# Every operation of a fused two-block transformer kernel gets a new place in its engine's queue

## What is computed

```
x = x + tanh(g0) * cross_attention(layernorm(x), ctx)        8 heads, rotary q and k, 128 context rows
x = x + tanh(g1) * bitlinear(relu(h)^2, w_proj)              h = bitlinear(ln(x), w_fc) + gate * low_rank(ln(x))
x = x + tanh(g2) * (ln(x) @ W1.T + mean(ctx) @ W2.T + b)
x = x + tanh(g3) * bitlinear(gelu(bitlinear(ln(x), w1, b1)), w2, b2)   activations rounded to 8 bits
```

## Time and profile before

| | |
|---|---|
| median of 3 runs | 1177.76 us (1174.64 to 1179.39) |
| span of the profiled execution, first to last instruction | 1176.7 us |
| PE, DVE, ACT, POOL busy, share of the span | 93%, 81%, 68%, 50% |
| chain that ended last: PE, ACT, DVE, POOL, issue, DMA | 55%, 17%, 16%, 5%, 4%, 2% |
| mean granted TensorE clock | 0.978 |

### The profile page before, as it was taken

The page is one execution under the profiler, slowest core; times in us unless marked ns, Lnnn a source line. Parts: engine busy times, 40 slices in busy tenths (PEclk is TensorE's granted clock), DMA queues, the critical chain, the costliest instruction groups (busy, mean ns, idle before and its releaser), DMA issues.

```text
span 1176.7 us, 22172 instructions
## 1 busy us (share of the span) xinstructions
PE 1094.3 (93%) x8270; PEld 677.4 (58%) x8558; DVE 953.5 (81%) x1989; ACT 799.4 (68%) x1575; POOL 591.5 (50%) x567
## 2 busy tenths in 40 slices
PE   5776699999999999999899999999999999999997
PEld 5544456474655656475655656475656656564654
DVE  4796868778789888788878798898879886998667
ACT  3988947676683958576584857676674957586545
POOL 4243545464653746454544656555545555564431
PEclk9888799999999999999999999999999999999999
DMA  9959651434525343533625252443436242432210
GB/s 339 367 153 309 204 122 47 99 81 77 126 59 117 69 116 73 104 81 68 126 53 136 57 123 68 89 110 77 108 55 145 45 119 61 103 69 55 68 45 27
DMA packets 273802, 128.11 MB, mean 109 GB/s; under 512 B 247568, under 2 KB 248080, under 8 KB 272016
## 3 DMA queue, kind: packets, MB, share of 16 engines
q1 hardware_dynamic: 273136, 125.73, 41.8%
q10 hardware_dynamic: 560, 0.96, 0.3%
HBM read 57.19 MB, written 8.39 MB: 56 GB/s over the span
## 4 chain that ended last, share of the span: by engine, by line
PE 55%; ACT 17%; DVE 16%; POOL 5%; issue 4%; DMA 2%; SPq 0%; ACTq 0%; DVEq 0%
PE ps L1861 14%; PE ps L1835 10%; PE ps L1904 6%; PE ps L1920 5%; PE ps L1788 5%; ACT e L966 4%; PE ps L1735 4%; PE ps L1883 4%; ACT rl L1002 3%; ACT hid L1007 2%; ACT sq L1013 2%; PE ps L1760 1%; DVE st L1369 1%; PE ps L1841 1%; PE ps L1775 1%
## 5 line engine op out<-in xcount | busy, mean ns | idle before, releaser
L1835 PE MATMUL ps<-xT,fcT 128*128 128x256 f16 x2048 | 262.5, 276 | 10.8 <-ACT rl L1002 7.1
L749 POOL TENSOR_TENSOR rs<-ve,nhalf 128x1 f32<-128x1 f32 x160 | 101.7, 638 | 306.1 <-DVE ve L1374 222.8
L1861 PE MATMUL ps<-pjT,hid 128*128 128x512 fp8e4 x1024 | 232.3, 379 | 2.6 <-POOL hid L776 1.6
L1835 PEld LDWEIGHTS ps<-xT,fcT 128*128 128x128 fp8e4 x2048 | 200.1, 99 | 52.6 <-ACT rl L1002 10.0
L776 POOL TENSOR_TENSOR hid<-sq,hid 128x512 f16<-128x512 f32 x128 | 163.1, 1279 | 80.3 <-ACT sq L1013 79.4
L1861 PEld LDWEIGHTS ps<-pjT,hid 128*128 128x128 f16 x1024 | 98.0, 98 | 98.3
L1002 ACT ACTIVATE rl<-ps,rsf 128x256 f32<-128x256 f32 x256 | 106.4, 469 | 25.0 <-PE ps L1841 24.8
L966 ACT ACTIVATE e<-ps,nmb,sig 128x128 f32<-128x128 f32 x256 | 113.1, 462 | 7.2 <-DVE nmb L1412 6.9
L1904 PE MATMUL ps<-w1T,q4T 128*128 128x512 fp8e4 x480 | 114.2, 379 | 0.7 <-issue 0.6
L1058 ACT ACTIVATE q<-h 128x2048 f16<-128x2048 f32 x30 | 57.3, 1910 | 79.3 <-DVE h L1531 79.3
L781 POOL TENSOR_TENSOR e<-e,einv 128x512 f32<-128x512 f32 x64 | 70.1, 1100 | 78.5 <-DVE einv L1416 78.5
(11 more groups left out here) (243 smaller groups left out, 2025.7 us busy)
## 6 DMA issues: line engine op xcount, KB each, us to landing
xb<-in_x SPq DMA_DIRECT2D x16, 512.0 KB, 3.6
xa<-in_x SPq DMA_DIRECT2D x15, 512.0 KB, 4.0
...
h<-in_w1T SPq DMA_DIRECT2D x6, 1024.0 KB, 5.8
h<-in_w2T SPq DMA_DIRECT2D x6, 1024.0 KB, 6.4
h<-in_wkvT SPq DMA_DIRECT2D x2, 1024.0 KB, 12.6
hid<-in_w_fc SPq DMA_DIRECT2D x2, 1024.0 KB, 9.9
```

Source lines behind the costliest of these rows:

```text
L1835: pe.matmul(ps[:, FFN0 + m % 2, a * G:(a + 1) * G], fcT[:, k, f * P:(f + 1) * P], xT2[:, xs, k, :], start=(xs == 0 and k == 0), stop=False)
L1861: mm = pe.matmul(ps[:, FFN0 + t, :], hid[:, xs, c, t * P:(t + 1) * P], pjT[:, c, :], start=(c == 0 and xs == 0), stop=(c == FC - 1 and xs ...
```

## The change

Every number in `ORDER` and `PREP` may be another; nothing else differs. No instruction, buffer or wait is added or removed. Counted over the queues of before and after: 340 of 658 operations of PE stand at another rank in their queue, 616 of 837 of DVE, 328 of 554 of ACT, 449 of 552 of POOL and 264 of 338 of SP. Most moves are by one to three ranks; `add_b2` on POOL moves by up to 26 and the load of b1 on SP by 28. The diff, cut to what the prediction speaks of:

```diff
@@ PE
-                s=((13,), (31,), (60,), (106,), (146,), (182,), (221,), (261,), (299,), (335,), (374,), (412,),
+                s=((13,), (31,), (61,), (105,), (146,), (183,), (220,), (261,), (300,), (337,), (373,), (412,),
...
-                    (173, 180, 183, 185, 186, 191, 192, 195), (212, 218, 220, 223, 224, 228, 230, 232),
+                    (173, 179, 181, 184, 185, 187, 192, 193), (212, 217, 222, 223, 225, 226, 227, 231),
...
-                    (331, 334, 340, 341, 342, 344, 346, 351), (370, 373, 378, 382, 383, 384, 385, 386),
+                    (331, 334, 339, 340, 345, 346, 347, 348), (370, 376, 378, 379, 380, 382, 385, 386),
...
-                w2=((92, 107), (132, 145), (170, 178), (210, 222), (247, 264), (288, 302), (326, 336), (364, 377),
+                w2=((91, 106), (131, 145), (170, 182), (210, 221), (247, 264), (287, 301), (327, 338), (366, 375),
@@ ACT
-                exp=((22, 23, 26, 27), (55, 56, 58, 60), (90, 98, 101, 102), (127, 128, 129, 134),
-                     (159, 160, 162, 167), (188, 190, 191, 192), (221, 222, 224, 226), (254, 255, 256, 261),
+                exp=((23, 24, 26, 27), (57, 58, 60, 63), (91, 92, 102, 103), (126, 127, 134, 135),
+                     (160, 161, 165, 167), (190, 191, 193, 194), (221, 222, 225, 229), (255, 256, 257, 263),
...
-                x2_hi=((50, 51), (84, 85), (113, 114), (144, 145), (176, 178), (207, 208), (240, 241), (272, 273),
+                x2_hi=((43, 54), (85, 86), (114, 115), (144, 145), (178, 179), (208, 209), (241, 242), (272, 273),
@@ POOL
-                add_b2=((57, 63), (93, 102), (123, 132), (155, 165), (195, 206), (222, 238), (261, 272), (295, 302),
-                        (329, 336), (363, 370), (398, 404), (427, 438), (461, 472), (501, 506), (527, 529),
+                add_b2=((67, 72), (108, 122), (141, 145), (171, 185), (209, 210), (245, 246), (264, 294), (297, 314),
+                        (340, 341), (364, 397), (398, 429), (431, 440), (469, 477), (507, 512), (528, 529),
@@ PREP
             PE=dict(x3_turn=(632, 634), q4_turn=(638, 642), q5_turn=(648, 649, 650, 651, 653, 654, 655, 656),
-                    k=(2, 3), v=(5, 6), low=(0,), mix=(14,), tern=(4, 10, 11, 15, 19, 20, 21, 22), low_t=(16,),
-                    row_scale=(24,), mean=(30,), spread=(1, 8, 12, 18, 25)),
+                    k=(2, 3), v=(5, 6), low=(0,), mix=(14,), tern=(4, 9, 11, 16, 18, 19, 20, 21), low_t=(23,),
+                    row_scale=(27,), mean=(30,), spread=(1, 10, 12, 15, 26)),
...
-                    thr=(9, 15, 20, 37, 46, 48, 49, 52), wo_max=(12,), v_top=(22,), wo_scale=(26,), wo_lo=(30,),
-                    mix_row=(43,), low_rank=(42,), v_parts=(28,), wx_max=(53,), hidden=(54,), wx_scale=(58,),
-                    wx_lo=(88,), row_scale=(56,), mean=(71,), diag=(55,), round=(72, 78, 81, 89, 90, 95, 97, 101),
-                    clip=(79, 85, 86, 91, 94, 98, 100, 103)),
+                    thr=(6, 13, 18, 34, 44, 45, 47, 48), wo_max=(20,), v_top=(24,), wo_scale=(25,), wo_lo=(29,),
+                    mix_row=(51,), low_rank=(39,), v_parts=(52,), wx_max=(50,), hidden=(55,), wx_scale=(67,),
+                    wx_lo=(88,), row_scale=(62,), mean=(70,), diag=(56,), round=(72, 73, 81, 86, 90, 91, 98, 102),
+                    clip=(76, 80, 87, 92, 94, 97, 114, 129)),
...
-                    evac=(6, 14, 15, 29, 33, 35, 36, 37), rows=(4, 7, 10, 21), whole=(5, 8, 12, 28), low=(32,),
-                    wx=(46,), sums=(39, 40, 41, 42, 43, 44, 45, 47), lift=(54, 61, 62, 67, 71, 76, 79, 80)),
+                    evac=(7, 14, 16, 30, 34, 35, 36, 37), rows=(4, 8, 10, 22), whole=(6, 11, 13, 29), low=(42,),
+                    wx=(53,), sums=(39, 40, 41, 44, 45, 46, 47, 49), lift=(55, 56, 64, 67, 74, 79, 81, 83)),
...
-            SP=dict(u=(0,), rows=(16,), ctx=(2,), wk=(3,), wq=(1,), wv=(7,),
-                    piece=(4, 5, 10, 18, 19, 15, 22, 24, 27, 29, 31, 32, 33, 36, 37, 38, 40, 41, 45, 47, 48, 50, 52, 55),
-                    wo=(6,), wc=(14,), wx=(13,), b1=(17,)))
+            SP=dict(u=(1,), rows=(15,), ctx=(0,), wk=(4,), wq=(2,), wv=(7,),
+                    piece=(3, 5, 9, 16, 14, 22, 21, 18, 26, 28, 30, 31, 32, 35, 36, 37, 38, 39, 43, 44, 46, 49, 52, 55),
+                    wo=(8,), wc=(20,), wx=(19,), b1=(45,)))
```

More of the change, by code:

```diff
@@ L336, in build @@
             PE=dict(
[L337 to L340, removed]
+                low_sum=((34,), (62,), (97,), (135,), (176,), (215,), (253,), (291,), (332,), (371,), (410,), (449,),
+                         (488,), (525,), (566,), (605,)),
@@ L341, in build @@
+                up_rest=((36, 37), (65, 66), (100, 102), (138, 139), (178, 180), (218, 219), (256, 258), (294, 295),
+                         (335, 336), (374, 377), (414, 415), (452, 453), (491, 493), (528, 529), (569, 570),
                          (608, 609)),
                 up=((32, 35, 38, 39, 40, 41, 42, 43), (63, 64, 67, 68, 69, 70, 71, 72),
[7 rows of a table removed]
[L350 removed]
[7 rows of a table removed]
[L358 to L359 removed]
@@ new lines, in build @@
+                wo=((24, 25), (54, 55), (89, 90), (125, 126), (165, 167), (204, 205), (242, 243), (282, 283),
+                    (318, 319), (360, 361), (399, 400), (438, 439), (478, 479), (518, 519), (557, 558), (594, 595)),
+                low=((33,), (60,), (95,), (133,), (174,), (211,), (251,), (289,), (330,), (369,), (408,), (447,),
+                     (486,), (524,), (564,), (603,)),
+                wx=((58, 59), (94, 108), (136, 147), (172, 186), (216, 224), (250, 267), (292, 304), (333, 341),
+                    (372, 381), (411, 418), (450, 457), (484, 497), (523, 538), (567, 575), (601, 606), (635, 636)),
@@ new lines, in build @@
+            ACT=dict(
+                low_part=((59,), (89,), (117,), (147,), (181,), (213,), (245,), (276,), (309,), (342,), (374,),
+                          (405,), (438,), (468,), (502,), (533,)),
+                up=((65, 66, 68, 69, 71, 72, 73, 77), (93, 94, 95, 96, 97, 98, 100, 101),
[7 rows of a table added]
+                x1_hi=((2, 3), (9, 12), (50, 51), (108, 116), (140, 148), (168, 180), (207, 210), (238, 243),
+                       (274, 275), (304, 305), (331, 337), (364, 369), (392, 402), (431, 434), (467, 471), (495, 496)),
+                rot=((15, 17), (48, 52), (87, 88), (121, 123), (155, 157), (185, 186), (216, 217), (248, 251),
+                     (283, 284), (312, 313), (344, 345), (376, 377), (407, 409), (440, 441), (477, 478), (501, 505)),
+                exp=((23, 24, 26, 27), (57, 58, 60, 63), (91, 92, 102, 103), (126, 127, 134, 135),
[3 rows of a table added]
+                p_hi=((25, 28, 31, 32), (61, 70, 75, 78), (99, 104, 105, 107), (128, 133, 137, 138),
[3 rows of a table added]
+                pv=((33, 38), (76, 80), (109, 110), (141, 142), (173, 174), (204, 205), (236, 237), (268, 269),
+                    (300, 301), (333, 334), (365, 366), (397, 398), (428, 429), (460, 461), (492, 493), (524, 525)),
+                x2_hi=((43, 54), (85, 86), (114, 115), (144, 145), (178, 179), (208, 209), (241, 242), (272, 273),
+                       (306, 307), (338, 339), (370, 371), (403, 404), (435, 436), (465, 466), (498, 499), (529, 531)),
+                low=((62,), (90,), (118,), (149,), (182,), (215,), (246,), (277,), (310,), (343,), (375,), (406,),
+                     (439,), (469,), (503,), (534,)),
+                x3_hi=((82, 84), (112, 124), (146, 151), (176, 187), (212, 218), (240, 247), (270, 279), (303, 314),
+                       (335, 347), (372, 379), (401, 411), (432, 442), (463, 470), (494, 506), (528, 532), (547, 548)),
+                gelu=((106, 113), (139, 150), (172, 177), (203, 211), (235, 244), (267, 278), (299, 308), (332, 340),
+                      (363, 368), (395, 400), (427, 433), (459, 464), (491, 500), (522, 527), (540, 545), (551, 552)),
+                q5=((111, 119), (143, 153), (175, 183), (206, 214), (239, 252), (271, 282), (302, 311), (336, 341),
+                    (367, 373), (399, 408), (430, 437), (462, 474), (497, 504), (526, 530), (543, 546), (553, 554))),
@@ new lines, in build @@
+            ACT=dict(q4_end=(549, 550), wq=(5,), k_hi=(18,), v_hi=(20, 21), tanh=(1,), wo=(19,),
+                     evac=(7, 14, 16, 30, 34, 35, 36, 37), rows=(4, 8, 10, 22), whole=(6, 11, 13, 29), low=(42,),
+                     wx=(53,), sums=(39, 40, 41, 44, 45, 46, 47, 49), lift=(55, 56, 64, 67, 74, 79, 81, 83)),
+            POOL=dict(whole=(19, 20, 21, 22), rot_k=(7, 8), csb=(13,), low_zero=(14,)),
+            SP=dict(u=(1,), rows=(15,), ctx=(0,), wk=(4,), wq=(2,), wv=(7,),
+                    piece=(3, 5, 9, 16, 14, 22, 21, 18, 26, 28, 30, 31, 32, 35, 36, 37, 38, 39, 43, 44, 46, 49, 52, 55),
+                    wo=(8,), wc=(20,), wx=(19,), b1=(45,)))
```

220 lines of the change are left out of this document (90 added, 130 removed), and 120 rows, old and new, of tables (down, exp, h, hid).

## The result

The changed kernel takes 1143.79 us in the median of 4 runs (1142.29 to 1145.46), the kernel before beside it 1178.58 (1174.64 to 1179.82): a ratio of 0.972, 95% interval 0.970 to 0.974. That is -34.8 us, where the prediction had -6.1 and a range that ended at 1158.

What follows compares the result with a forecast made beforehand. It took TensorE as the bound, with work in 932.80 of 960 us after 180 us. Setup -2.3 and steady stretch -3.8 made -6.1: 1171.7 us, with 1158 to 1187 as the range for 8 in 10.

Steps and rivals of the forecast that it cites:

- The ceiling: After 180 us: TensorE's open time, 27.2 of 960 us, is about all that any order could give back.
- The steady term, -3.8: After 180 us: four of TensorE's waits go, -5.7 us, with a third taken as lost to new holes.
- The four waits: TensorE's waits at s(5), s(8), low_sum(4) and up(4,5), predicted to give -1.3, -2.0, -1.1 and -1.3 us.
- its bound of +5.7: Steady stretch, slow end: moved work opens new holes twice as large as the waits it closes, +5.7 us.
- The rival with the port, -18.9, chance 0.12: Shared-port collisions of VectorE and GpSimd vanish, with TensorE's waits for them: -18.9 us, 1158.9; chance 0.12.
- no table of one queue's order ties its times to the other's: VectorE's and GpSimd's shared port: issue order decides who waits, so changed orders need not keep collisions apart; no size given.
- Slower by add_b2, +7.7: GpSimd's late add_b2 holds VectorE's x4 2.5 us in four places; with the setup +7.7 us, 1185.5; chance 0.21.
- The wash, 1175.5: Steady stretch: holes close and open alike, 0.0 there, -2.3 us in the setup, 1175.5; chance 0.22.
- Setup, -2.3: First 180 us: 0.0 up to up(0,0), -2.0 and -0.3 after it; -2.3 us, between -8 and +6.
- the -2.0 of one lift and -0.3: Setup, 116 to 180 us: one lift less between ScalarE's up pieces, -2.0; x1(1,1) before ln3(0,1) on VectorE, -0.3.
- wx and wc behind piece 7: Setup, SP queue: later loads of wx and wc delay mix by 0.4 us, up to 4 with a fuller DMA.
- The 1.1 us around a span: Whole kernel: the median of the runs lies 1.1 us above the span, added to 1170.6 for the forecast.

Runs made afterwards that it cites:

- The cut kernels: Kernels before and after, each with most of GpSimd's arithmetic cut to 16 of 512 columns, all its instructions kept: 1161.75 and 1142.96 us.
- all five queues together, behind the seam: The kernel before, with the new order in all queues only from about 190 us, where both orders have done the same operations: 1160.84 us (0.988).

## Why the prediction was wrong

- **The ceiling.** "27.2 us is about all that any order could give back" after 180 us. 22.7 of it came back (27.2 to 4.5), and 6.5 more from the busy time of the same 7414 multiplies behind q(2). The multiplies' ends are modelled, so a wait too short to show can stand inside the busy time; that is the likely source of most of the 6.5, and the granted clock, 0.99 against 1.00, of a part. Neither was separated. So the open time is no ceiling of what can be won.
- **The steady term, -3.8.** This is the step that failed. It measured -29.1. The four waits that made it up are worth nothing alone (+2.5), because work moved into one hole opened another, as the prediction feared in its bound of +5.7: 3.52 us at w2(2,1). "In the rest of the 27.2 us the order is about as before or the comparison says nothing" stood in the place of nearly the whole gain, some 2 us a group in the mean. It was put at nothing because the waits of TensorE alone can't price it. A third lost was a choice with nothing under it.
- **The rival with the port, -18.9, chance 0.12.** Its mechanism was right for a little under half: 15.4 us of before are GpSimd's doing, and after has lost all but 0.8 of it. That its 18.9 lies near the 18.8 that isn't GpSimd's is chance. The argument against it was a misreading: "'s median of 802 is near its minimum". The mean in the same trace was 993, and the means and totals are what went with the end time, not the medians. "Most of the delay before s is the row's turn in VectorE's queue" was right as a reason why order matters, and was put on the wrong side.
- **"no table of one queue's order ties its times to the other's".** The rule of the Trainium skill, page "SBUF — State Buffer", section "Who interferes with whom", holds here: two inputs in SBUF collide, one of them in PSUM does not (674 to 694 ns in after). The conclusion drawn from it failed: with nothing but the orders changed, the collisions fell by 24 of 76 us. The likely reason, argued and not shown, is that both queues hang on the same results of ScalarE and TensorE, so that their orders set what lies beside what.
- **Slower by add_b2, +7.7.** In the source view of after, x4 (L1539) waited for that addition 2.4 us in 2 places, not 10 in four (before, nobody waited for it). The mechanism exists and is small; the earlier trace rows's median of 1263 is 1268, with a longest of 1809 that collided:

```profile
L777 POOL TENSOR_TENSOR r<-r,b2bc x30: 1260/1268/1809, 196.7 to 1067.4; 128x512 f32<-128x512 f32 x30
...
  DVE r L1539: 2.4, 2
```

- **The wash, 1175.5.** Its sign, open time near 27, is refuted by 4.5.
- **Setup, -2.3.** Measured -4.2 against the profiled execution, -1.2 against executions whose setup ran early: the number is inside its bounds either way, and within the spread of that yardstick. wo(0) was to begin at 88.5; the first row shows it. The second is mean, the third the first up piece:

```profile
88.98 5.34 PE L1771 MATMUL ps<-wo,qT 128*128 128x512 f16 x24 [0.51 <-DVE qT L1365]
...
110.50 0.60 PE L1704 MATMUL ps<-wsum,ones 128*128 128x8 f32 x2 [5.28 <-ACT hT L924]
...
119.52 1.87 PE L1818 MATMUL ps<-xT,fcT 128*128 128x256 f16 x8 [3.89 <-DMA xT<-x16f]
```

  The gain up to wo(0) was right, and that it is swallowed too, only by more: up(0,0) came at 119.5 and not at 116.3. ScalarE's sums had to wait for pieces to land, which the prediction did not price:

```profile
102.52 1.91 ACT L924 ACTIVATE h<-h 128x2048 f32<-128x2048 f32 x1 [2.61 <-DMA h<-in_w2T]
...
105.96 1.91 ACT L924 ACTIVATE h<-h 128x2048 f32<-128x2048 f32 x1 [1.44 <-DMA h<-in_w2T]
```

  Between up(0,0) and q(2) 7.4 us came back (54.10 to 46.73), not the -2.0 of one lift and -0.3. Windows of before and of after:

```profile
116.33:170.43 54.10, 44.19 (x266) 26.64 (x275) 42.77 (x58) 41.72 (x82) 24.03 (x18) 0.84 0.61 156
119.52:166.25 46.73, 41.46 (x267) 25.28 (x276) 36.25 (x50) 36.64 (x74) 22.78 (x18) 0.90 0.73 214
```

  2.7 us of it are busy time of TensorE, beside a granted clock of 0.90 where before had 0.84, a term that the prediction didn't have. Of the pieces of up, where two had waited 1.47 and 2.69, these did, 2.3 us less:

```profile
135.78 1.05 PE L1818 MATMUL ps<-xT,fcT 128*128 128x256 f16 x8 [1.60 <-ACT rl L985]
...
140.11 1.05 PE L1818 MATMUL ps<-xT,fcT 128*128 128x256 f16 x8 [0.23 <-ACT rl L985]
```

  wx and wc behind piece 7: mix began at 60.94, 0.5 later than in the earlier trace rows, against a predicted 0.4.
- **The 1.1 us around a span.** In every run behind the prediction a kernel's time lies 2.0 to 2.2 us above its span (1145.46 against 1143.4), so half of that distance was taken for the spread of the runs. It makes 1 us.

So the sum was -2.3 - 3.8 and should have been about -4 for the setup and -29 behind it. The cause falls into two parts of like size: collisions, with GpSimd's own time, 14.6 (15.4 against 0.8), and what stays between the orders without them, 18.8, called fit here because collisions and VectorE's total are ruled out for it. Two things stay open. The cut kernels remove GpSimd's time as well as its collisions; that both together are worth little is shown for after (0.8), how they divide in before is not. And which moves carry the 18.8 isn't known: only all five queues together, behind the seam, gave a part of the gain (-15.6).
